# A four-layer graph network on one core: three 128x128 transposes taken from TensorE and done by VectorE blocks and a trip through HBM

## The reference

```python
# layer 0: out = max over columns of relu(W1 x + ...), W1 = W2 = adj
x = layernorm(x + L0(x, adj, adj, b))
# layer 1 (attention over adj): h = x @ W; e = leaky_relu(s1 + s2); e = e * adj
#   att = softmax(e); out = elu(att @ h + beta * h)
x = layernorm(x + L1(x, W, a, beta, adj))
# layer 2: out = (adj @ x) @ weight + bias
x = layernorm(x + L2(x, adj, weight, bias))
# layer 3: 8 heads of 64
q = x @ Wq + bq; k = x @ Wk + bk; v = x @ Wv + bv
scores = q k^T / sqrt(64) + mask(adj == 0)
weights = softmax(scores); out = weights @ v
x = layernorm(x + out)
```

## Time and profile before

| | us |
|---|---|
| median of the runs (3) | 2746.28 |
| lowest, highest | 2746.2, 2747.28 |
| the profiled execution, device time | 2746.01 |
| its span in the trace | 2744.2 |
| PE busy | 2677.5 |
| PEld busy | 2404.0 |
| DVE busy | 1925.9 |
| ACT busy | 1474.4 |
| POOL busy | 1483.6 |

### The profile page before, as it was taken

One profiled execution on the slowest core, in us unless ns is written; L12 is line 12 of the kernel. 1 busy time (PEld: TensorE's weight loads), 2 busy tenths in 40 slices (PEclk: granted clock), 3 DMA queues, 4 the chain that ended last, 5 costly groups with the idle time before them and its releaser, 6 DMA issues.

```text
span 2744.2 us, 60531 instructions
## 1 busy us (share of the span) xinstructions
PE 2677.5 (98%) x19593; PEld 2404.0 (88%) x19593; DVE 1925.9 (70%) x6165; ACT 1474.4 (54%) x4360; POOL 1483.6 (54%) x1806
## 2 busy tenths in 40 slices
PE   4899999999999999999999999999999999999996
PEld 3799899889889889989988988988998998898896
DVE  7777776776777776777767767767777777767753
ACT  3355555555555555555555555555555555555554
POOL 5655555555555555555555555555556555555541
PEclk9999999999999999999999999999999999999998
DMA  4000000000000000000000000000000000000000
GB/s 124 15 22 28 28 24 27 27 24 27 24 27 27 19 29 30 20 27 31 19 27 31 20 27 31 20 27 31 20 27 27 24 27 27 24 27 27 13 16 24
DMA packets 41607, 75.19 MB, mean 27 GB/s; under 512 B 5584, under 2 KB 5712, under 8 KB 41424
## 3 DMA queue, kind: packets, MB, share of 16 engines
q1 hardware_dynamic: 41424, 73.49, 8.3%
HBM read 39.92 MB, written 33.55 MB: 27 GB/s over the span
## 4 chain that ended last, share of the span: by engine, by line
PE 96%; DVE 1%; issue 1%; ACT 1%; DMA 0%; POOL 0%; ACTq 0%; SPq 0%; POOLq 0%; DVEq 0%
PE rot L796 24%; PE rot L798 23%; PE rot L797 23%; PE score L917 5%; PE rot L904 5%; PE rot L853 4%; PE rot L889 4%; PE rot L939 2%; PE rot L952 2%; PE rot L873 2%; PE rot L877 2%; PE s_bank L861 0%; PE att_bank L945 0%; DMA probs<-in_L_gnn_W 0%; DVE x L644 0%
## 5 line engine op out<-in xcount | busy, mean ns | idle before, releaser
L338 POOL TENSOR_TENSOR ve<-mv,eps_col 128x1 f32<-128x1 f32 (+1 forms) x448 | 88.1, 197 | 695.5 <-ACT e L503 352.8
L796 PE MATMUL rot<-w_hi,y_hi 128*128 128x512 f32 x1024 | 425.2, 415 | 5.6 <-DVE y_lo L634 4.7
L360 POOL TENSOR_TENSOR x2b<-x,bias 128x512 f32<-128x512 f32 x128 | 203.5, 1590 | 416.4 <-DVE x L644 416.4
L798 PE MATMUL rot<-w_hi,y_lo 128*128 128x512 f32 x1024 | 404.8, 395 | 0.0
L797 PE MATMUL rot<-w_lo,y_hi 128*128 128x512 f32 x1024 | 404.2, 395 | 0.0
L549 ACT ACTIVATE probs<-score,sc_nmax 128x128 f32<-128x128 f32 x1024 | 357.0, 371 | 11.4 <-DVE sc_nmax L757 11.4
L796 PE MATMUL rot<-xt_hi,wk_hi 128*128 128x256 f32 x1024 | 299.8, 293 | 0.0
L634 DVE TENSOR_TENSOR y_lo<-rot,y_hi 128x512 fp32r<-128x512 f32 x128 | 88.5, 691 | 296.4 <-ACT y_hi L467 296.4
L798 PE MATMUL rot<-xt_hi,wk_lo 128*128 128x256 f32 x1024 | 290.2, 283 | 0.0
L798 PE MATMUL rot<-xt_hi,wq_lo 128*128 128x256 f32 x1024 | 289.8, 283 | 0.0
L797 PE MATMUL rot<-xt_lo,wq_hi 128*128 128x256 f32 x1024 | 289.7, 283 | 0.0
(11 more groups left out here) (117 smaller groups left out, 7758.5 us busy)
## 6 DMA issues: line engine op xcount, KB each, us to landing
x_in<-in_x SPq DMA_DIRECT2D x128, 256.0 KB, 2.6
out_x<-x SPq DMA_DIRECT2D x128, 256.0 KB, 2.2
probs<-in_L_gnn_W SPq DMA_DIRECT2D x1, 1024.0 KB, 8.0
v_sb<-in_L_gnn_weight SPq DMA_DIRECT2D x1, 1024.0 KB, 7.1
probs<-in_L_gnn_Wv SPq DMA_DIRECT2D x1, 1024.0 KB, 5.4
v_sb<-in_L_gnn_Wq SPq DMA_DIRECT2D x1, 1024.0 KB, 5.3
probs<-in_L_gnn_Wk SPq DMA_DIRECT2D x1, 1024.0 KB, 5.4
x<-in_L_gnn_a SPq DMA_DIRECT2D x1, 512.0 KB, 5.7
```

Source lines behind the costliest of these rows:

```text
L360: pool.tensor_tensor(x2b[:, :], x2[:, slot.buf(L_GCN, 2), :], bias2[:, :], ALU.add)\
L796: pe.matmul(outp, lh, rh, start=first, stop=False)
L798: return pe.matmul(outp, ll, rh, start=False, stop=last)
```

## The change

The three transposes that feed or follow layer 3's attention leave TensorE. In their place stands the same sequence three times, for `probs` (1024 columns), x3 and `o_t` (512 columns each):

1. DVE transposes each 32x32 block where it stands (`dve.transpose`), into `probs_b`, `x3_b` and `o_t`.
2. SP issues four DMAs (`scatter`), one for each group of 32 partitions, that write each row of each block, 32 floats or 128 bytes, to its place in an HBM scratch tensor.
3. SP waits until the four have landed and issues one DMA (`gather`) that reads the scratch back as tiles of 128 rows of 512 bytes, into `probs_t`, `xt_f` and `o_norm`.

ACT's two copies to `probs_t` go; DVE's copy to `o_t` becomes the block transpose. `xt_hi` and `xt_lo` are now made from `xt_f` in SBUF. `probs` has one buffer for the exponentials, the other is `probs_b`. The scaling of `o_norm` and POOL's addition move to the next slot (lag `L_ON` = 8). On PE, y1 now stands ahead of the q projection. On ACT, y1_hi and z0 stand ahead of q, the exponential of layer 1 ahead of k, and the two groups of four exponentials ahead of `xt_hi` and ahead of the rounding of x. On DVE, the eight masked minima are split in two groups around layer 0's small steps, the dot products of layer 1 move to the start of the next slot, and x3, the statistics of layer 3 and `o_t` move within the slot.

```diff
+BLOCK = 32
+SCATTER = 16 * (P // BLOCK)
+L_ON = L_PV + 1
...
+        x3_b = sb("x3_b", [P, FEATS])
+        xt_f = sb("xt_f", [P, KC, P])
+        probs_b = probs[:, 1, :, :, :].rearrange("p c t n -> p (c t n)")
...
@@ sync @@
+            def scatter(hbm, blocks, landed):
+                for a in range(P // BLOCK):
+                    rows = slice(a * BLOCK, (a + 1) * BLOCK)
+                    sp.dma_start(hbm.rearrange("n (b r) p -> r (n b) p", r=BLOCK)[:, :, rows],
+                                 blocks[rows, :].rearrange("r (m c) -> r m c", c=BLOCK)).then_inc(landed, 16)
+            def gather(tiles, hbm, landed):
+                sp.dma_start(tiles, hbm.rearrange("n q p -> q n p")).then_inc(landed, 16)
...
             def emit(slot):
+                if slot.on(L_PV):
+                    slot.wait(sp, probs_b_done, L_PV)
+                    scatter(pt_hbm, probs_b, pt_scattered)
+                if slot.on(L_PV):
+                    slot.wait(sp, pt_scattered, L_PV, each=SCATTER)
+                    gather(probs_t[:, :, :, :].rearrange("p c t n -> p (c t) n"), pt_hbm, pt_in)
                 if slot.on(L_LOAD):
...
+                if slot.on(L_TR):
+                    slot.wait(sp, x3_b_done, L_TR)
+                    scatter(xt_hbm, x3_b, xt_scattered)
+                if slot.on(L_TR):
+                    slot.wait(sp, xt_scattered, L_TR, each=SCATTER)
+                    gather(xt_f[:, :, :], xt_hbm, xt_in)
                 if slot.on(L_OUT) and slot.part(L_OUT) == GROUP - 1:
...
+                if slot.on(L_PV):
+                    slot.wait(sp, x4_done, L_PV, 1)
+                    slot.wait(sp, o_t_done, L_PV)
+                    scatter(ot_hbm, o_t, ot_scattered)
+                    slot.wait(sp, ot_scattered, L_PV, each=SCATTER)
+                    gather(o_norm[:, :, :].rearrange("p g (c e) -> p (g c) e", e=P), ot_hbm, ot_in)
...
@@ scalar @@
-                    act.activation(probs_t[:, 0, :, :].rearrange("p t n -> p (t n)"), rot[3][:, :], ACT.Copy)\
-                        .then_inc(pt0_done, 1)
...
-                    act.activation(probs_t[:, 1, :, :].rearrange("p t n -> p (t n)"), rot[0][:, :], ACT.Copy)\
-                        .then_inc(pt1_done, 1)
...
+                if slot.on(L_QK):
+                    slot.wait(act, probs_b_done, L_QK, 1)
+                    slot.wait(act, inv_done, L_QK, 2)
+                    exponentials(slot, 0)
...
-                    slot.wait(act, xt_mm, L_TR)
+                    slot.wait(act, xt_in, L_TR, each=16)
...
+                if slot.on(L_QK):
+                    exponentials(slot, 1).then_inc(score_exp, 1)
                 round_x(Slot(slot.base, slot.offset + 1))
...
@@ vector, first in emit @@
+                if slot.on(L_PV):
+                    slot.wait(dve, score_exp, L_PV)
+                    slot.wait(dve, pt_scattered, L_PV, 1, SCATTER)
+                    dve.transpose(probs_b[:, :], probs[:, 0, :, :, :].rearrange("p c t n -> p (c t n)"))\
+                        .then_inc(probs_b_done, 1)
+                if slot.on(L_ATT):
+                    dot_products(slot)
...
+                if slot.on(L_ON):
+                    slot.wait(dve, ot_in, L_ON, each=16)
+                    slot.wait(dve, inv_done, L_ON)
...
+                    slot.wait(dve, xt_scattered, L_TR, 1, SCATTER)
+                    dve.transpose(x3_b[:, :], x3[:, t2, :]).then_inc(x3_b_done, 1)
...
-                    dve.tensor_copy(o_t[:, :], rot[3][:, :]).then_inc(o_t_done, 1)
...
+                if slot.on(L_QK):
+                    slot.wait(dve, score_mm, L_QK)
+                    slot.wait(dve, score_exp, L_QK, 1)
+                if slot.on(L_PV):
+                    slot.wait(dve, pv_mm, L_PV)
+                    slot.wait(dve, ot_scattered, L_PV, 1, SCATTER)
+                    dve.transpose(o_t[:, :], rot[3][:, :]).then_inc(o_t_done, 1)
+                if slot.on(L_QK):
+                    masked_minimum(0)
...
@@ tensor @@
-                        ins = pe.transpose(rot[3][:, t * P:(t + 1) * P], probs[:, par, 0, t, :], ident[:, :])
...
-                        ins = pe.transpose(rot[0][:, t * P:(t + 1) * P], probs[:, par, 1, t, :], ident[:, :])
...
-                    slot.wait(pe, pt0_done, L_PV)
-                    slot.wait(pe, pt1_done, L_PV)
+                    slot.wait(pe, pt_in, L_PV, each=16)
+                    slot.wait_last(pe, (v_done, L_V, 1), (o_t_done, L_PV, 1))
...
-                        ins = pe.transpose(rot[3][:, n * P:(n + 1) * P], o_t[:, n * P:(n + 1) * P], ident[:, :])
...
-                        ins = pe.transpose(rot[2][:, k * P:(k + 1) * P], x3[:, slot.buf(L_TR, 2), k * P:(k + 1) * P],
-                                           ident[:, :])
```

More of the change, by code:

```diff
@@ L355, in emit @@
             def emit(slot):
+                if slot.on(L_ON):
+                    k, first = slot.part(L_ON), slot.buf(L_ON, BUFS) // GROUP * GROUP
+                    slot.wait(pool, o_norm_done, L_ON)
+                    if k == 0:
+                        slot.wait(pool, x4_init, L_ON - (GROUP - 1))
+                    res = x4[:, first:first + GROUP, k * CHUNKS * P:(k + 1) * CHUNKS * P]
+                    pool.tensor_tensor(res, res, o_norm[:, :, :], ALU.add).then_inc(x4_done, 1)
                 if slot.on(L_GCN):
@@ L436, in biased, with exponentials @@
                 return act.activation(dst, src, ACT.Identity, bias=bias)
+            def exponentials(slot, h):
+                par = slot.buf(L_QK, 2)
+                act.wait_ge(score_nmax_done, slot.graph(L_QK) * 2 + h + 1)
+                for c in range(CHUNKS):
+                    for g in range(GROUP):
+                        t, i = g * 2 + h, (g * CHUNKS + c) * 2 + h
+                        ins = act.activation(probs[:, 0, c, t, :], score_tile(c, g, h),
+                                             ACT.Exp, bias=sc_nmax[:, c, t:t + 1], scale=-1.0,
+                                             accum_out=sc_sum[:, par, i:i + 1])
+                return ins
             def round_x(slot):
@@ L454, in emit @@
                         .then_inc(v_done, 1)
-                if slot.on(L_QK):
-                    slot.wait(act, q_mm, L_QK)
-                    slot.wait(act, score_mm, L_QK, 1)
-                    for c in range(CHUNKS):
-                        chunk = slot.part(L_QK) * CHUNKS + c
-                        ins = biased(q_sb[:, c, :], q_bank(c), qb_col[:, chunk:chunk + 1])
-                    ins.then_inc(q_done, 1)
                 if slot.on(L_GAT):
@@ L475, in emit @@
                 if slot.on(L_QK):
+                    slot.wait(act, q_mm, L_QK)
+                    slot.wait(act, score_mm, L_QK, 1)
+                    for c in range(CHUNKS):
+                        chunk = slot.part(L_QK) * CHUNKS + c
+                        ins = biased(q_sb[:, c, :], q_bank(c), qb_col[:, chunk:chunk + 1])
+                    ins.then_inc(q_done, 1)
+                if slot.on(L_ATT):
+                    slot.wait(act, att_nmax_done, L_ATT)
+                    slot.wait(act, att_n_done, L_ATT, 2)
+                    act.activation(att_p[:, b2, :], att_e[:, b2, :], ACT.Exp, bias=att_nmax[:, b2:b2 + 1],
+                                   accum_out=att_sum[:, b2:b2 + 1]).then_inc(att_exp, 1)
+                if slot.on(L_QK):
                     slot.wait(act, k_mm, L_QK)
@@ L777, in emit @@
                 if slot.on(L_GAT):
-                    aggregate("1", g2)
+                    slot.wait(dve, r1_sum_done, L_GAT)
+                    statistics("1", r1[:, g2, :])
                 if slot.on(L_GCN):
@@ L855, in emit @@
                     ins.then_inc(y1_mm, 1)
+                if slot.on(L_QK):
+                    weight_split(slot, "wk", L_QK)
+                    if slot.part(L_QK) == 0:
+                        slot.wait(pe, xt_lo_done, L_QK - (GROUP - 1))
+                    slot.wait_last(pe, (edge_max_done, L_EDGE, 1), (q_done, L_QK, 1))
+                    projection(rot[0], "wq", slot).then_inc(q_mm, 1)
                 if slot.on(L_ATT):
@@ L934, in emit @@
                         ins.then_inc(setup_mm, 1)
-                if slot.on(L_PV):
-                    slot.wait(pe, o_t_done, L_PV)
-                    for n in range(GROUP * CHUNKS):
-                        ins = pe.transpose(rot[3][:, n * P:(n + 1) * P], o_t[:, n * P:(n + 1) * P], ident[:, :])
-                    ins.then_inc(ot_mm, 1)
                 if slot.on(L_ATT):
```

208 lines of the change are left out of this document (74 added, 134 removed).

## The result

The changed kernel takes 2789.3 us (median of four runs, 2788.3 to 2790.8), the kernel before 2746.6 in the same comparison: the ratio is 1.0156, with a 95% interval of 1.0138 to 1.0173. The forecast was 2575 us and faster. The time lies in its range; its sign is wrong.

The account below looks back on a forecast made before the run. The probabilities' closed loop through HBM, 19.2 us a slot, was taken to bound just above PE's 18.97: 2746 less 128 x (20.73 - 19.2), 196 us, plus 25 us fill and drain gave 2575 us; range 2525 to 2950 us.

Parts of the forecast that it names:

- PE alone is the bound: PE's slot: four groups of four transposes leave it, 1.76 us, so 20.73 us becomes 18.97.
- Price of a packet: DMA through HBM: a 128-byte packet costs 15 ns of engine time, ends 10 and 28; 12.6 us a slot.
- The trip: Probabilities' way through HBM: scatter 5.3 us plus gather 3.7 us, together 9.0 us.
- The rest of the loop: From PV's start on PE to the end of DVE's block transpose of `probs`: 10.2 us.
- PE stays the bound: Rival: packets cost 10 ns or so, PE bounds with a slot of 18.97 us; 2546 us, chance 0.12.
- Block transposes 0.6 and 1.15 us: New DVE work: 0.6 us for x3's 512 columns, 1.15 us for the 1024 of `probs`.
- The other trips cost nothing: Trips of x3 and `o_t` through HBM: 6.2 us each, no cost at 15 ns a packet.
- DVE held by `ot_in`: Sign: the cause if PE waits elsewhere than at PV, at z1 for `y1_lo` or y2 for x2.
- Fill and drain: Start and last slots, where trips stand in the open: +25 us, ends 10 to 35.
- ACT loses two copies of 0.59 us: ACT: loses these copies, gains nothing, is 54% busy; so no term in the sum.
- its matmuls follow each other without a gap: PE's timeline before the change: a slot takes 20.73 us, its matmuls gapless.
- the slow rival: Rival: 128-byte HBM writes cost 28 ns, the loop outlasts today's slot at 22.6 us; 3010 us, chance 0.34.

Follow-up runs that it names:

- c1: a1 with DVE's loop cut moved from ahead of the block transpose of `probs` to behind `y1_lo`, order of work unchanged: 2562.8 us, ratio 0.9336.
- d2: a1 with 66 one-column memsets in DVE's start-up, so that its loop starts at instruction 636 instead of 570: 2565.2 us, ratio 0.9344.
- c2: a1 with the scatter of the probabilities issued twice, the second into another scratch, the gather waiting for both: 3196.9 us, ratio 1.1642.
- a1: The changed kernel with `y2_hi` moved ahead of the output's two normalisations (line 559) on ACT: 2698.1 us, ratio 0.9825.
- d4: The changed kernel with 66 one-column memsets on DVE ahead of its loop and nothing else: 2693.3 us, ratio 0.9809.
- f1: The kernel before with 66 one-column memsets on DVE ahead of its loop, moved from instruction 562 to 628: 2748.2 us, ratio 1.0009.

## Why the prediction was wrong, step by step

- *PE alone is the bound, 1.76 us leave its slot.* Right once the two causes named below are gone: in c1 and d2 the slot is 19.0 us; the forecast for PE alone was 18.97.
- *Price of a packet, 15 ns with ends of 10 and 28.* The DMA share of d2 is 58.5% of 2563.6 us, over 16 engines and 1382864 packets 17.4 ns on average for the mix; the forecast's 12.6 us in a slot are 18.7 ns for it. A 128-byte piece alone can be read from c2 against a1: 64.5% of 3188.6 us less 55.5% of 2696.5, over 16 engines, for 532480 packets more is about 17 ns each (an estimate). The line between two far rows held. By the forecast's doubled price, 30 ns for a piece, a scatter would take 9.2 us by its formula, and the four are done in 4.45. So the rule that it cites from the Trainium skill (DMA: Bandwidth & Descriptors, Specifications), a read-modify-write below 512 bytes, shows no doubling in these runs.
- *The trip.* Forecast 5.3 + 3.7, measured 4.45 + 4.0. *Issue.* 0.56 us for a scatter where 0.35 to 0.45 stood: inside its ends.
- *The rest of the loop.* Forecast 10.2 us; in d2 from PV's start (1405.90) to the end of the block transpose (1415.94) it is 10.0. The loop is 10.0 + 8.5 = 18.5 us, 0.5 less than PE's slot. So of the two nearly level cases the rival *PE stays the bound* is right for c1 and d2: 2546 was said, 2563 to 2565 measured. That the forecast's own 2575 lies nearer is luck: its loop was too long by 0.7 us and its fill and drain too short by 15.
- *Block transposes 0.6 and 1.15 us.* Measured 0.712 and 1.220 (rows below). Small.
- *The other trips cost nothing.* Right while the pipeline is full: in d2 DVE waits 14.1 us in 6 for `ot_in`, all of it behind 2400 us, and ACT 10.9 us in 4 for `xt_in`, 10.7 of it ahead of 300. The forecast's sign for waits elsewhere, DVE held by `ot_in`, pointed at the wrong place: PE did wait elsewhere, for `y2_lo` and `s_col`, and DVE waited for `ot_in` only 12.3 us in 7, in the drain.
- *Fill and drain +25 us.* Before it is 2746.3 - 128 x 20.73 = 93 us, in d2 2565.2 - 128 x 19.0 = 133: +40, above the end of 35.
- *"ACT loses two copies of 0.59 us"*, *"no term"*. **This step failed.** It read ACT's busy share, 54%, and not its order. The change moved `o_norm` and the addition by a slot; the forecast followed the result of this trip to DVE, but not on to the statistics, POOL and ACT, and not to what is queued behind line 559 there. The runs show in its place that ACT stands for `out_shift` (2.09 us in the slot above) with `y2_hi` queued behind it, and PE waits 93.0 us in 63 for `y2_lo`. Price: 91 to 128 us (a1 against the changed kernel, d2 against d4). The forecast's own list of signs asks what a late DVE would hold up ("y2 for x2"); the same question was not asked of ACT.
- *The turn of the loop.* **This failed too**, as a term that is missing: *"its matmuls follow each other without a gap"* is right of the kernel before, and from it the slot was taken as free of other costs after the change as well. Nothing in the earlier trace rows shows the turn. The trace of before did hold it: 158 instruction packets, by the 24 that are left in f1 some 5 for each turn, and 296 us of DVE idle time at the place that the change fills. Price: 96 us in the changed kernel (d4), 133 in a1.
- *Waiting priced by its length.* The forecast never gave a wait a tail. In a1 27 turns cost 133 us and only 93.2 - 16.1 = 77 us of it is waiting for `s_col`. The other 56 us are about what the lower clock takes: the mean granted clock is 0.961 over 2696.5 us in a1 and 0.981 over 2563.6 in d2, which lacks 105 and 49 us of the full clock (an estimate).

2789 us is therefore the forecast's machine with two defects of 224 us together, and neither is in the transposes, the packets or HBM, on which the slow rival and the range's upper end were built. That the range holds the time is luck: the reason isn't among its cases.

## What to carry to other kernels

When a step moves by a slot, follow it through every queue to its last consumer, and for each in-order engine write down what is queued behind the waiting instruction; an output that nobody on the core needs belongs behind everything that somebody needs. Before work is put behind a loop's jump, count the instruction packets and "issue" waits: some packets per turn mean that the turn fetches code and may stall the engine, and if its idle time covers that today, the move can uncover it; a few dozen harmless instructions ahead of the loop then test, and may cure, it. If a change is slower though its own mechanism works, list the waits of the bounding engine and remove the largest one by one and together, since what they cost doesn't add up. Here the kernel went from 1.6% slower to 6.7% faster with one reordered copy and 33 memsets.

## What the runs showed of the hardware that was not expected

- A turn of DVE's loop stalls it for 2.3 to 2.8 us and then 1.0 in the mean (62 to 76 and 27 to 28 us in 27), with five 8 KB fetches, or not at all, by the place of the code (table above).
- PE, busy without a gap before, gets half its clock by the end of one wait of 3.04 us, and keeps it for about 6 us of gapless work (a1).
- DVE's block transposes of fp32 take 1.22 us for 1024 columns and 0.71 for 512 (groups by line, shapes apart; busy us, mean ns; idle before). The one from PSUM (`o_t`) has the same 712 ns as that from SBUF:

```profile
L681 DVE STREAM_TRANSPOSE probs<-probs 128x1024 f32<-128x1024 f32 x128 | 156.1, 1220 | 67.8 <-issue 62.4 <-ACT probs L493 5.3
L737 DVE STREAM_TRANSPOSE x_b<-x 128x512 f32<-128x512 f32 x128 | 91.1, 712 | 15.0
```

- Two operations on DVE have a longer mean after the change, but a mean hides two sorts here. The one that writes x3 (L652 before, L733 after) goes from 550 to 720 ns in the mean and only from 542 to 546 in the median: in the changed kernel it takes 1.16 us in every fourth slot and 0.53 to 0.55 in the others. The one that writes `att_e` (L659 before, L708 after, 847 to 1037 ns) takes 0.28 us at its shortest and over 1 us in other slots, before the change too: at 1389.16 in the kernel before it takes 1.35 us and ends 0.14 us behind an operation of POOL on SBUF (1388.93, 1.44 us). POOL's powers on 128x1 (L343 before, L391 after) go from 552 to 741 ns. That the two engines hold each other up there was not tested.
